# Four stages of a modulated convolution with a low-rank linear layer: the setup of the kernel is reordered in five places, and one wait of the main loop is split

## What is computed

```python
s = style @ mw.T + mb                                    # style: 64 numbers a sample
weight = SCALE * w * s[:, None, :, None]
demod = rsqrt(sum(weight * weight, axis=(2, 3)) + EPS)
out = conv(x, weight * demod[:, :, None, None]) + b      # same, upsample+blur, same, blur+downsample
```

```python
A_eff = einsum('bn,nri->bri', gate, lora_A)              # 8 blocks x 32 x 512
B_eff = einsum('bn,nor->bor', gate, lora_B)
```

## Time and profile before

| | before |
|---|---|
| median of 3 runs | 1113.19 us |
| the profiled execution | 1112.61 us |
| its span (first to last instruction) | 1110.8 us |
| PE busy | 1069.1 us, 96% |
| DVE / POOL / ACT busy | 504.9 / 507.1 / 331.3 us |
| matrix products, weight loads | 22064 each |
| end of the setup's block | about 92 us into the span |

### The profile page before, as it was taken

How to read it: one execution, slowest core, us unless ns; L and a number is a source line. 1 busy time by engine, 2 the same in 40 slices (tenths; PEclk the granted TensorE clock), 3 DMA queues, 4 the chain that set the end, 5 groups by cost and what they waited for, 6 DMA issues and landing times.

```text
span 1110.8 us, 47494 instructions
## 1 busy us (share of the span) xinstructions
PE 1069.1 (96%) x22064; PEld 794.4 (72%) x22064; DVE 504.9 (45%) x1244; ACT 331.3 (30%) x721; POOL 507.1 (46%) x380
## 2 busy tenths in 40 slices
PE   5899999999999999999999999999999999999997
PEld 4457777776777777777777777777777777777775
DVE  5774443543444344544343345544344345534353
ACT  2323323234322322323332224223222333323321
POOL 2536745345535552465435452655442543744500
PEclk9799999999999999999999999999999999999999
DMA  4535400002334200002123300002115200000211
GB/s 142 191 129 217 155 3 2 3 3 69 116 100 141 70 3 3 2 2 69 41 81 114 107 12 2 3 2 59 52 60 143 70 3 3 2 3 23 58 40 38
DMA packets 30084, 64.92 MB, mean 58 GB/s; under 512 B 5632, under 2 KB 6720, under 8 KB 27968
## 3 DMA queue, kind: packets, MB, share of 16 engines
q1 hardware_dynamic: 28352, 61.51, 17.7%
q10 hardware_dynamic: 1536, 0.39, 0.2%
HBM read 44.05 MB, written 17.83 MB: 56 GB/s over the span
## 4 chain that ended last, share of the span: by engine, by line
PE 84%; DVE 4%; ACT 2%; issue 1%; DVEq 0%
PE bank_b L1570 16%; PE bank_a L1570 15%; PE bank_a L108 10%; PE bank_b L108 10%; PE bank_a L91 5%; PE bank_b L91 5%; PE bank_b L79 3%; PE bank_a L79 3%; PE bank_a L67 2%; PE bank_b L67 2%; DVE y3t_lo L1313 2%; ACT y3t_hi L1184 2%; PE bank_b L1518 1%; PE bank_a L1518 1%; PE bank_a L1580 1%
## 5 line engine op out<-in xcount | busy, mean ns | idle before, releaser
L1131 POOL TENSOR_TENSOR xs<-x,tab 128x512 f32<-128x512 f32 x96 | 110.9, 1164 | 368.3 <-DVE x L1321 368.3
L1118 POOL TENSOR_TENSOR sums<-raw 128x896 f32<-128x896 f32 x62 | 128.3, 2090 | 35.2 <-ACT raw L1171 35.2
L108 PE MATMUL bank_a<-y,wv 32*64 32x256 f32 x4096 | 116.2, 375 | 0.5 <-issue 0.5
L108 PE MATMUL bank_b<-y,wv 32*64 32x256 f32 x4096 | 116.0, 375 | 0.1
L1570 PE MATMUL bank_b<-w_hi,y3t_hi 128*128 128x512 f32 x256 | 104.8, 409 | 3.9 <-ACT y3t_hi L1184 1.6
L1570 PE MATMUL bank_a<-w_hi,y3t_hi 128*128 128x512 f32 x256 | 104.7, 409 | 2.4 <-DVE y3t_lo L1313 1.1
L108 PEld LDWEIGHTS bank_a<-y,wv 32*64 32x64 f32 x4096 | 94.7, 130 | 15.1 <-issue 1.8
L108 PEld LDWEIGHTS bank_b<-y,wv 32*64 32x64 f32 x4096 | 93.9, 130 | 16.1 <-issue 1.9
L1570 PE MATMUL bank_b<-w_lo,y3t_hi 128*128 128x512 f32 x256 | 100.4, 392 | 0.0
L1570 PE MATMUL bank_a<-w_lo,y3t_hi 128*128 128x512 f32 x256 | 100.4, 392 | 0.0
L1321 DVE TENSOR_TENSOR x<-bank_a,x 128x512 f32<-128x512 f32 x64 | 43.5, 690 | 102.9 <-PE bank_a L1570 75.3
(11 more groups left out here) (297 smaller groups left out, 1868.3 us busy)
## 6 DMA issues: line engine op xcount, KB each, us to landing
w_hi<-w_scratch SPq DMA_DIRECT2D x36, 256.0 KB, 3.2
w_lo<-w_scratch SPq DMA_DIRECT2D x36, 256.0 KB, 3.2
x_in<-in_x SPq DMA_DIRECT2D x32, 256.0 KB, 4.6
out_x<-x SPq DMA_DIRECT2D x32, 256.0 KB, 2.4
w_raw<-in_w SPq DMA_DIRECT2D x3, 1024.0 KB, 9.0
w_scratch<-w_hi SPq DMA_DIRECT2D x3, 1024.0 KB, 4.1
w_scratch<-w_lo SPq DMA_DIRECT2D x3, 1024.0 KB, 7.0
w_raw<-w_scratch SPq DMA_DIRECT2D x2, 1024.0 KB, 10.4
```

The source lines that it names most:

```text
L108: last = pe.matmul(banks[b][2 * CH * h:2 * CH * (h + 1), HALF * u:HALF * (u + 1)], keep["wv"][rows, a, SPAN - q:SPAN - q + 2].rearrange("p ...
L1118: g_.tensor_tensor(sums[i][:], pairs[:, :, one[0], one[1]:one[1] + SPAN], pairs[:, :, other[0], other[1]:other[1] + SPAN], ALU.add).then_i ...
L1131: nc.gpsimd.tensor_tensor(xs[:, b, 1:LEN + 1], src[:, b], column(n, T_S, b).broadcast_to((P, LEN)), ALU.mult).then_inc(xs_ready, 1)
```

## The change

- **Taps.** `cw` and `cw_late` are issued from ACT's queue as its first instructions; ACT waits for each only ahead of the squares that read it. On SP `mod_b` moves ahead of `cond_r`, and `conv_b` behind the loads of `x`.
- **Variances in two steps.** PE signals `mod_done` after `mod_v` and again after `mod_r`. DVE adds the biases of `mod` and `mod_v`, writes `T_S`, makes the two part products of the down taps, and only then waits for `mod_r`. ACT squares `mod` and `mod_v` first (`square_ready` 1) and `mod_r` afterwards (`square_ready` 2); PE makes all variances of L779 first, then those of L783. `table_r` and `T_P` move behind the read of the variances.
- **Gated products.** The 512 rows to be contracted are laid out otherwise: partition = expert x 8 ranks, so one contraction of 128 rows holds all 16 experts. `gmat` is 128 x 64 (8 ranks x 8 blocks) and is the same for all rank groups. Four products of 128 rows by 64 columns take the place of eight of 128 by 128, nothing is accumulated, and two products fill the two column halves of a bank. The scratch tensors are rank by block instead of block by rank, so that a main-program load of one block reads 32 rows with a stride.
- **Bias products.** `bias3` goes round the four column quarters in each of its four steps, instead of finishing one quarter first.
- **turn.** PE waits for the first two tiles of `y3` ahead of the first two transposes, and for all of them ahead of the other two; before, it waited for all at once.

```diff
@@ SP
-                ("cond_r", cond_r, io["cond_r"]), ("mod_w4", mod_w4, io["mod_w4"]), ("mod_b", mod_b[:], io["mod_b"]),
-                ("cw", cw[:], io["cw"][:, 0:2]), ("cw_late", cw_late[:], io["cw"][:, 2:4]), ("conv_b", conv_b[:], io["conv_b"]),
+                ("mod_b", mod_b[:], io["mod_b"]), ("cond_r", cond_r, io["cond_r"]), ("mod_w4", mod_w4, io["mod_w4"]),
@@ ACT
-            act.wait_ge(loaded["cw"], 16)
-            act.wait_ge(loaded["cw_late"], 16)
+            for name, dst, src in (("cw", cw[:], io["cw"][:, 0:2]), ("cw_late", cw_late[:], io["cw"][:, 2:4])):
+                act.dma_start(dst, src).then_inc(loaded[name], 16)
             for k in range(CONVS):
+                if k % 2 == 0:
+                    act.wait_ge(loaded["cw_late" if k else "cw"], 16)
                 a.activation(sq[:, :, k], (cw if k < 2 else cw_late)[:, k % 2], ACT.Square).then_inc(squares, 1)
+            act.wait_ge(mod_ready, 3)
+            a.activation(mod_sq[:, :, 0:3 * GR].rearrange("p l (k f) -> p l k f", k=3), mod[:, :, 0:3, 1], ACT.Square)
+            a.activation(mod_sq[:, :, 3 * GR:V_R], mod_v[:].rearrange("p l u f -> p l (u f)"),
+                         ACT.Square).then_inc(square_ready, 1)
             act.wait_ge(mod_ready, 3 + LAYERS)
...
             a.activation(mod_sq[:, :, V_R:VARS], mod_r[:, :, 1], ACT.Square).then_inc(square_ready, 1)
@@ POOL
-            for kk in range(4):
-                g.tensor_tensor(gmat[:, kk], gate_t[:, kk].unsqueeze(2).broadcast_to((P, 8, R2)),
-                                delta[:].unsqueeze(1).broadcast_to((P, 8, R2)), ALU.mult).then_inc(gm_ready, 1)
+            g.tensor_tensor(gmat[:], gate_t[:].unsqueeze(1).broadcast_to((P, RB, 8)),
+                            delta[:].unsqueeze(2).broadcast_to((P, RB, 8)), ALU.mult).then_inc(gm_ready, 1)
@@ DVE: after mod and mod_v
+            dve.wait_ge(mod_ready, 3)
...
+            v.tensor_copy(table[:, :, :, T_S], m(0, 0)).then_inc(scale_ready, 1)
+
+            dve.wait_ge(loaded["cw_late"], 16)
+            for i, f in enumerate(DOWN_FACTORS):
+                ins = v.tensor_scalar(part_dn[:, :, :, i], cw_late[:, 1], f, None, ALU.mult)
+            then(ins)
+            dve.wait_ge(mod_done, 2)
             for l in range(LAYERS):
                 v.tensor_tensor(mod_r[:, l], mod_r_ps[l], wide(mod_b4[:, l, 1:4], SAMPLES),
                                 ALU.add).then_inc(mod_ready, 1)
@@ DVE: after the read of the variances
+            dve.wait_ge(mod_ready, 3 + LAYERS)
+            product(table_r[:, :, 0], mod_r[:, :, 0], 0.25 * SCALE, mod_r[:, :, 1])
+            then(v.tensor_tensor(table[:, :, :, T_P], m(1, 0), m(2, 0), ALU.mult))
+            v.tensor_scalar(table[:, :, :, T_P], table[:, :, :, T_P], 0.25 * SCALE, None, ALU.mult)
@@ PE
-                    for h in range(2):
-                        for parity in range(2):
-                            at = CH * (2 * h + parity)
-                            out = bias3_ps[l][at:at + CH]
-                            pe.matmul(out[:, 0], gq[:, l, 0], gam[:, h], start=True, stop=True, skip_group_check=True)
-                            for e in range(2):
-                                last = pe.matmul(out[:, 1 + e], eq[:, l, parity, e], eps[:, h],
-                                                 start=True, stop=(e != parity), skip_group_check=True)
-                                if e == parity:
-                                    last = pe.matmul(out[:, 1 + e], gq[:, l, 1 + e], gam[:, h], start=False, stop=True,
+                    for step in range(4):
+                        for h in range(2):
+                            for parity in range(2):
+                                at = CH * (2 * h + parity)
+                                out = bias3_ps[l][at:at + CH]
+                                if step == 0:
+                                    last = pe.matmul(out[:, 0], gq[:, l, 0], gam[:, h], start=True, stop=True,
                                                      skip_group_check=True)
+                                elif step == 2:
+                                    last = pe.matmul(out[:, 1 + parity], gq[:, l, 1 + parity], gam[:, h],
+                                                     start=False, stop=True, skip_group_check=True)
+                                else:
+                                    e = parity if step == 1 else 1 - parity
+                                    last = pe.matmul(out[:, 1 + e], eq[:, l, parity, e], eps[:, h],
+                                                     start=True, stop=(step == 3), skip_group_check=True)
...
+            last.then_inc(mod_done, 1)
             pe.wait_ge(loaded["cond_r"], 16)
...
-            pe.wait_ge(mod_ready, 3 + LAYERS)
+            pe.wait_ge(mod_ready, 3)
...
+            pe.wait_ge(square_ready, 2)
+            for l in range(LAYERS):
                 for r in range(ROWS):
                     rows = slice(CH * r, CH * (r + 1))
                     last = pe.matmul(var_r_ps[rows, l], sq[rows, l, 2, 0], mod_sq[rows, l, V_R:VARS],
...
-            g2 = gmat[:].rearrange("p k b r -> p k (b r)")
+            g2 = gmat[:].rearrange("p r b -> p (r b)")
...
                 for h in range(2):
-                    for kk in range(4):
-                        last = pe.matmul(banks[h][:], g2[:, kk, h * P:(h + 1) * P], raw_[:, kk],
-                                         start=(kk == 0), stop=(kk == 3))
+                    for c in range(2):
+                        last = pe.matmul(banks[h][8 * RB * c:8 * RB * (c + 1)], g2, raw_[:, 2 * h + c],
+                                         start=True, stop=True)
                     last.then_inc(done, 1)
@@ turn
-                pe.wait_ge(y3_act, tiles(m, ROWS))
-                pe.wait_ge(y3_dve, tiles(m, ROWS))
...
                 for j in range(ROWS):
                     half, block = j // 2, j % 2
+                    pe.wait_ge(y3_act, tiles(m, 2 * half + 2))
+                    pe.wait_ge(y3_dve, tiles(m, 2 * half + 2))
```

More of the change, by code:

```diff
@@ L18 @@
 E1, R1 = 8, 16
-R2 = 32
+R2, RB = 32, 8
 E3, R3 = 4, 8
@@ L517, in _ @@
                             ALU.add).then_inc(mod_ready, 1)
-            for l in range(LAYERS):
-                v.tensor_tensor(mod_r[:, l], mod_r_ps[l], wide(mod_b4[:, l, 1:4], SAMPLES),
-                                ALU.add).then_inc(mod_ready, 1)
-            dve.wait_ge(mod_ready, 3 + LAYERS)
+            dve.wait_ge(mod_ready, 3)
             LAYER_0, LAYERS_LATE = slice(0, 1), slice(1, LAYERS)
@@ L540, in _ @@
             v.tensor_copy(table[:, :, :, T_S], m(0, 0)).then_inc(scale_ready, 1)
-            product(table_r[:, :, 0], mod_r[:, :, 0], 0.25 * SCALE, mod_r[:, :, 1])
-            then(v.tensor_tensor(table[:, :, :, T_P], m(1, 0), m(2, 0), ALU.mult))
-            v.tensor_scalar(table[:, :, :, T_P], table[:, :, :, T_P], 0.25 * SCALE, None, ALU.mult)
+            dve.wait_ge(loaded["cw_late"], 16)
             for i, f in enumerate(DOWN_FACTORS):
@@ L547, in _ @@
             then(ins)
+            dve.wait_ge(mod_done, 2)
+            for l in range(LAYERS):
+                v.tensor_tensor(mod_r[:, l], mod_r_ps[l], wide(mod_b4[:, l, 1:4], SAMPLES),
+                                ALU.add).then_inc(mod_ready, 1)
             for tap, ((t0, f0), *rest) in enumerate(DOWN):
@@ L1749, in host_layout, with by_rank @@
     b0 = c(i["L0_ffn_Bf"].transpose(0, 2, 1)).reshape(2, P, LEN).transpose(1, 0, 2)
-    a2 = i["L2_ffn_lora_A"][..., order].reshape(4, P, LEN).transpose(1, 0, 2)
-    b2 = c(i["L2_ffn_lora_B"].transpose(0, 2, 1)).reshape(4, P, LEN).transpose(1, 0, 2)
+    def by_rank(m):
+        return m.reshape(P // RB, R2 // RB, RB, LEN).transpose(0, 2, 1, 3).reshape(P, R2 // RB, LEN)
+    a2 = by_rank(i["L2_ffn_lora_A"][..., order])
+    b2 = by_rank(i["L2_ffn_lora_B"].transpose(0, 2, 1))
     x = i["x"].reshape(GROUPS, ROWS, ROWS, CH, LEN).transpose(0, 1, 3, 2, 4).reshape(GROUPS, P, ROWS, LEN)
```

26 lines of the change are left out of this document (12 added, 14 removed).

## The result

The changed kernel takes 1107.11 us, median of 4 runs (1103.73 to 1108.72), beside 1113.13 for the kernel before: ratio 0.9935, 95% interval 0.9918 to 0.9952. Forecast were 1096.0 us and a range of 1091 to 1103. The direction was right. Of the 17.2 us, 6.0 came by the medians, 8.9 in the profiled execution (1103.73, span 1101.6). A second series of six runs gave 1106.79, ratio 0.9948 (0.9932 to 0.9965).

The account below looks back on a forecast made before the run. PE, busy in nearly all of the 1110.8 us span, was taken as the bound. 16.3 us from an earlier main-program start plus 0.9 in turn made 17.2: 1112.61 became 1095.4, with 0.6 to the median 1096.0 us; range 1091 to 1103.

Parts of the forecast that it names:

- Taps delay `mod_w` by 0.5, bounds 0 and 2.2: Setup's start: the taps' 768 KB beside cond and mod_w delay PE's start by 0.5 us, bounds 0 and 2.2.
- The rest of the front: Setup to 34 us: variances read at 21.2, 6.5 us earlier; first convolution's evacuation 5.2 us earlier, bounds 3.7 to 6.5.
- `bias3` of layer 0, 0.9 gained: Setup, 34 to 62 us: layer 0's bias products gain 0.9 us, bounds 0 to 1.4.
- Four quarters at once: Bias products: four column quarters overlap, 0.93 us a layer instead of 2.0; late layers 3.0 us instead of 6.0.
- Rival A: Full-row quarters and column halves don't overlap further; PE's setup ends 5.1 us later, 1101.1 us; chance 0.14.
- `late_ready` moves by the front's 6.1: Setup: SP's as2 and bs2 loads behind late_ready move 6.1 us earlier, so L854 starts at 60.8.
- The wait of 2.5 leaves the clock: Setup, behind b2's products: PE idles 2.5 us for as2 and bs2; the forecast charged no clock loss.
- rival B: The new 2.5 us idle stretch halves PE's clock for 6.6 us, costing 3.3 us; 1099.3 us; chance 0.11.
- From `inner_tiles` to the main program, 7.5: Setup's end: inner_tiles 1.8 us, late bias3 3.0, outer_tiles 2.1, then 0.5 to the main program, starting at 75.9.
- SP's end at 75.4 beside PE's 75.3: Setup's end: SP's last store lands at 75.4, PE ends at 75.3, two nearly equal ends.
- `turn`, 0.9 and no cost: Main program: last phase's first transposes start 0.9 us earlier; six added waits a phase cost 0, bound 1.9 us.
- Rival E: Each new wait in turn drains PE's queue; 0.23 us at 96 boundaries costs 22 us, 1118 us; chance 0.03.

Follow-up runs that it names:

- the gated products alone: The kernel before with only the new gated products of a2 and b2: median 1108.9 us, ratio 0.9945 to the kernel before.
- the one with the stores held: Changed kernel with taps and POOL's adds delayed, mod_w4 third, own as2/bs2 buffers; SP holds x loads and b2/w2 stores until late bias products finish: 1105.90 us.
- `turn` alone: The kernel before with only the split waits of turn: median 1113.07 us, ratio 0.9989 to the kernel before.
- the bias products alone: The kernel before with only the bias products going round the quarters: median 1109.09 us, ratio 0.9959 to the kernel before.
- the kernel with POOL's adds behind `late_ready`: The changed kernel, but POOL waits for late_ready before its four adds of the bias to x: ratio 0.9901.

## Why the prediction was wrong, by its own steps

- **Taps delay `mod_w` by 0.5, bounds 0 and 2.2.** Wrong: 3.1 us, beyond the bound. That bound counted the taps' bytes at full rate, and was too small: `cond`, which is issued ahead of `mod_w`, landed at 4.7 instead of 2.9 as well. "Need only get its share" was argued, not read from a row. This is the term mis-sized at the front: with it gone, `mod_r` ends at 14.02.
- **The rest of the front.** The last variance products took 2.63 us instead of 1.9 and waited for ACT's square; the read ended at 23.95 instead of 21.2. The three table writes took 1.1 (1.3 said), the evacuation came 3.5 us earlier (5.2 said, bound 3.7). The first convolution took 5.6 us (5.8 before).
- **`bias3` of layer 0, 0.9 gained.** Right: 2.5 to 1.3 us. **Four quarters at once.** Right: 2.9 to 3.3 us for three layers against 6.0 where no pause falls into them, and alone too. Rival A fell. The rule weighed in the prediction (the Trainium skill, "TensorE: Matmul & The Clock Gate", Part 3) would have kept 6.0; the trace has eight records in 0.42 to 0.44 us.
- **`b2`'s products in 1.9.** Right: 1.94 for 8 records.
- **`late_ready` moves by the front's 6.1.** This step failed most. It moved by 1.45. The front gave 4.35, and DVE was held twice: in `wv`, 1.96 us instead of 1.09 (rows below), and in L585, 2.37 instead of 0.33. I had moved the chain as a block, and hadn't asked what POOL would run beside DVE once its release had moved. So L866 starts at 65.32, not 60.8: 4.5 us.

```profile
47.85 1.96 DVE L688 SCALAR_TENSOR_TENSOR wv<-sums 128x896 f32<-128x896 f32 x1
```

```profile
52.21 1.09 DVE L683 SCALAR_TENSOR_TENSOR wv<-sums 128x896 f32<-128x896 f32 x1
```

(Changed kernel first, the kernel before second.) In eleven of the fifteen traces the layer-0 bias products go round the quarters; in ten of these `wv` starts inside POOL's first add for `w0` and takes 1.64 to 1.99 us. In the four with the old order, and in the eleventh, it starts within 0.2 us of that add's end and takes 1.09. So on this chain the quicker `bias3` gives back most of what it gains. No run removed this hold by itself.

- **The wait of 2.5 leaves the clock.** This was rival B, at 0.11 and 3.3 us. It came with a wait of 5.2 and cost 3.5 us in L866 and 1.3 in `bias2`: `inner_tiles` starts 12.5 us after the shared products instead of 7.6. Even a wait of 2.3 did it, in the gated products alone. The clue was the earlier trace rows: 0.11 was too low a chance for what the same trace shows behind a wait of 4.0.
- **From `inner_tiles` to the main program, 7.5.** Measured 8.4: the two parts of L79 above with the pause between them, the first sign of the instruction fetch. As 1.8 + 3.0 + 2.1 it was right but for that.
- **SP's end at 75.4 beside PE's 75.3.** PE set the end in every trace but the one with the stores held.
- **`turn`, 0.9 and no cost.** Right. Rival E fell: the distances of the other phases are the same within 0.4 us but for slips that stand at other places in each run.
- **The sum.** 4.5 (1.75 front and 2.9 DVE held, by the rows 0.1 more) + 4.9 (clock) + 0.9 = 10.3 of the missing 10.4. What the profiled run gained beyond 5.9 is `turn`'s 1.0 and the main program's slips: it is 3.3 us shorter than before, in the other traces between 3.9 shorter and 3.4 longer, whatever the edit.

The 8.9 us of the profiled execution flatter the change: it is the fastest of its four runs.

Open: what takes the clock when PE doesn't wait, as in `turn` alone and the bias products alone. That was seen and not tried.

## What to carry to other kernels

When a long product is made short, the chain that it covered comes onto the path: follow that chain instruction by instruction, and ask which engine is now released beside it. Sum the parts only where nothing of one runs beside another; here 15 us in parts (10 by the starts in the profiles) were 6 in one. A short wait on PE can cost more behind it than it lasts, so price the products behind it at half clock as well, and check that filling or removing it pays.

## What the runs showed that I had not expected

- PE's instructions travel by the same DMA engines as the data, 16 KB at a time. Beside SP's transfers at 400 GB/s: pauses of 1.0, 2.3, 3.3 and 3.5 us, marked "issue". They appear where many small products follow each other while large stores run.
- A write of 96 elements a partition on DVE can take 1.2 us instead of 0.2, when POOL works beside it. The same happens in the main program, at other places in each trace; how much of the difference between equal runs it makes was not counted. The phase near 445 us of the kernel with POOL's adds behind `late_ready`, beside the same phase of the changed kernel:

```profile
443.49 5.03 POOL L1162 TENSOR_TENSOR x<-x,ob 128x512 f32<-128x512 f32 x4
...
445.18 3.51 DVE L1281 TENSOR_TENSOR y_e<-y,mask 128x32 f32<-128x32 f32 x2
...
448.74 0.28 PE L121 MATMUL bank_b<-y_e,up_e 128*32 128x16 f32 x8 [1.71 <-DVE y_e L1281]
```

```profile
446.74 2.20 DVE L1280 TENSOR_TENSOR y_e<-y,mask 128x32 f32<-128x32 f32 x2
```

Two tiny products of 32 elements last 3.51 us, until the adds of POOL have ended, PE waits 1.71, and the clock from 449.2 to 453.7 is 0.62 in the mean: the phase is 2.9 us longer than in the kernel before. One such slip is half of what the whole change gained.
